# Turning the quantised GELU rows by DMA on SyncE's queue, with the second product one step later

## The reference, cut to what matters

```python
def activation_quant(x):
    scale = 127.0 / jnp.clip(jnp.max(jnp.abs(x), axis=-1, keepdims=True), EPS_Q)
    return jnp.clip(jnp.round(x * scale), -128, 127) / scale
def bit_linear(x, w, b, dim_in):
    x_norm = simple_rms_norm(x, dim_in)
    x_q = activation_quant(x_norm)
    w_q = weight_quant(w)                       # sign(w) * mean(abs(w))
    return jnp.einsum('bsd,od->bso', x_q, w_q) + b
h = bit_linear(x, w1, b1, DIM)
h = jax.nn.gelu(h, approximate=False)
return bit_linear(h, w2, b2, INNER)
```

## Time and profile before

| | us |
|---|---|
| median of 3 runs | 2112.15 (2109.58 to 2112.73) |
| the profiled execution | 2108.11 |
| its span, first to last instruction | 2106.3 |
| PE busy in the span | 1942.6 (92%) |
| VectorE busy | 1350.0 (64%) |
| ScalarE busy | 1079.6 (51%) |
| GpSimd busy | 431.5 (20%) |

### The profile page before, as it was taken

One profiled execution on the slowest core, in us unless ns is written; L12 is line 12 of the kernel. 1 busy time (PEld: TensorE's weight loads), 2 busy tenths in 40 slices (PEclk: granted clock), 3 DMA queues, 4 the chain that ended last, 5 costly groups with the idle time before them and its releaser, 6 DMA issues. The chain is left out here.

```text
span 2106.3 us, 30642 instructions
## 1 busy us (share of the span) xinstructions
PE 1942.6 (92%) x10514; PEld 1486.9 (71%) x10514; DVE 1350.0 (64%) x2408; ACT 1079.6 (51%) x2590; POOL 431.5 (20%) x515
## 2 busy tenths in 40 slices
PE   6999789999999999969999999999979978886898
PEld 5888667777777777757887778778768855553444
DVE  6777577777777777744424655554745438885886
ACT  4333266666766666652314321121324329994998
POOL 1111144444444444410000000000000002222111
PEclk9999899999999999989999999999999989997999
DMA  6776853333332330146433221223287422331121
GB/s 251 262 261 218 297 155 110 82 91 91 101 89 83 100 80 23 31 137 228 145 100 130 60 60 40 61 61 107 94 294 247 149 82 96 116 101 51 33 59 45
DMA packets 209028, 253.76 MB, mean 120 GB/s; under 512 B 12246, under 2 KB 158822, under 8 KB 202476
## 3 DMA queue, kind: packets, MB, share of 16 engines
q1 hardware_dynamic: 208876, 251.82, 37.2%
HBM read 151.10 MB, written 100.68 MB: 120 GB/s over the span
## 5 line engine op out<-in xcount | busy, mean ns | idle before, releaser
L971 ACT ACTIVATE at_prob<-at_S,at_bias,at_rq 128x384 f32<-128x384 f32 (+1 forms) x256 | 185.2, 733 | 131.5 <-DVE at_bias L1058 124.3
L1069 DVE TENSOR_TENSOR at_pt_lo<-at_PT,at_pt_hi 128x512 fp32r<-128x512 f32 x224 | 154.8, 692 | 84.6 <-ACT at_pt_hi L978 84.6
L835 POOL TENSOR_SCALAR at_prob<-at_prob,at_rsum 128x384 f32<-128x384 f32 (+1 forms) x256 | 161.4, 643 | 148.9 <-DVE at_rsum L1064 148.8
L1722 ACT ACTIVATE gu_silu<-gu_G 128x512 f32<-128x512 f32 x64 | 38.1, 597 | 242.7 <-PE gu_G L103 233.0
L1049 DVE TENSOR_REDUCE at_nmax<-at_S 128x1 f32<-128x384 f32 (+1 forms) x256 | 152.7, 619 | 6.6 <-PE at_S L885 2.3
L978 ACT ACTIVATE at_pt_hi<-at_PT 128x512 fp32r<-128x512 f32 x224 | 134.9, 603 | 42.3 <-PE at_PT L892 42.3
L1759 DVE TENSOR_TENSOR gu_h<-gu_silu,gu_U 128x512 f32<-128x512 f32 x64 | 43.9, 688 | 150.9 <-PE gu_U L103 104.0
L892 PE MATMUL at_PT<-c_ident,at_prob 128*128 128x128 f32 x896 | 126.0, 275 | 3.5 <-DVE at_pt_lo L1069 3.5
L824 POOL TENSOR_TENSOR at_q<-at_by_cos,at_by_sin 128x512 f32<-128x512 f32 x64 | 82.4, 1288 | 215.3 <-DVE at_qv L1044 183.3
L881 PE MATMUL at_S<-at_k_hi,at_q_hi 128*128 128x384 f32 (+1 forms) x256 | 109.7, 428 | 7.5 <-DVE at_q_lo L1074 7.5
L892 PEld LDWEIGHTS at_PT<-c_ident,at_prob 128*128 128x128 f32 x896 | 100.3, 140 | 22.4 <-DVE at_pt_lo L1069 14.2
(11 more groups left out here) (341 smaller groups left out, 5470.8 us busy)
## 6 DMA issues: line engine op xcount, KB each, us to landing
wide<-at_ot SPq DMA_DIRECT2D x64, 256.0 KB, 2.9
wide<-gu_h SPq DMA_DIRECT2D x64, 256.0 KB, 3.3
o_a<-wide SPq DMA_DIRECT2D x14, 1024.0 KB, 4.8
d_a<-wide SPq DMA_DIRECT2D x13, 1024.0 KB, 8.6
keys_hi<-kv_kt_hi SPq DMA_DIRECT2D x16, 512.0 KB, 3.2
keys_lo<-kv_kt_lo SPq DMA_DIRECT2D x16, 512.0 KB, 4.2
values_hi<-kv_v_hi SPq DMA_DIRECT2D x16, 512.0 KB, 4.8
values_lo<-kv_v_lo SPq DMA_DIRECT2D x16, 512.0 KB, 5.1
```

Source lines behind the costliest of these rows:

```text
L835: pool.tensor_scalar(prob[u % 2][:, h, 0:n], prob[u % 2][:, h, 0:n], rsum[:, s:s + 1], 1.0, ALU.mult, ALU.mult).then_inc(normed.sem, 1)
L971: act.activation(prob[u % 2][:, h, 0:n], S[h][:, 0:n], ACT.Exp, bias=bias[:, s:s + 1], scale=rq[u % 4][:, h:h + 1], accum_out=sums[:, s:s ...
L1069: dve.tensor_tensor(pt_lo[f % 4][:], bank_of("p", u, kb)[:], pt_hi[f % 4][:].bitcast(F32), ALU.subtract).then_inc(pt_done.sem, 1)
```

## The change

The rows of hq are no longer transposed on TensorE and copied out by ScalarE. SyncE issues a transposing DMA from hq to hqt (512 KB) for each tile, as the last item of its step, on tile s-2. `second_product` moves from tile s-2 to s-3, `finish` from s-3 to s-4, and `store_y` stays at s-4. xb gets eight rooms instead of four, used by the turn's parity, with a wait for the y that last read the room. The banks HT and their counters go.

```diff
-        xb = mem.sb("xb", [P, TT, D])
+        xb = mem.sb("xb", [P, 2 * TT, D])
-        HT = [mem.bank(f"HT{i}", (P, 1024), BF16) for i in range(2)]
-        HT_full = mem.counter("HT_full", 2 * TT)
-        ht_done = mem.counter("ht_done", 2 * TT)
+        hq_turned = [mem.counter(f"hq_turned{t}", 16) for t in range(TT)]
+        def xb_room(turn, t):
+            return xb[:, turn % 2 * TT + t, :]
 # SyncE
+            def turn_h(turn, t):
+                sp.wait_ge(*hq_done.at(turn, t + 1))
+                sp.wait_ge(*Y_full.at(turn, t + 1 - TT))
+                sp.dma_start_transpose(hqt[:, t, :, :], hq[:, t, :]).then_inc(hq_turned[t].sem, 16)
                 for a in back(4):
                     store_y(*a)
+                for a in back(2):
+                    turn_h(*a)
 # TensorE
-            def turn_h(turn, t):
-                pe.wait_ge(*hq_done.at(turn, t + 1))
-                for a in range(2):
-                    pe.wait_ge(*ht_done.at(turn, 2 * t + a - 1))
-                    for i in range(8):
-                        j = 8 * a + i
-                        last = pe.transpose(HT[a][:, i * P:(i + 1) * P], hq[:, t, j * P:(j + 1) * P], c.ident_bf[:])
-                    last.then_inc(HT_full.sem, 1)
             def second_product(turn, t):
                 pe.wait_ge(*y_done.at(turn, t))
+                pe.wait_ge(*hq_turned[t].at(turn, 16))
                 for k in range(IC):
-                    if k % 8 == 0:
-                        pe.wait_ge(*ht_done.at(turn, 2 * t + k // 8 + 1))
-                for a in back(2):
-                    turn_h(*a)
-                for a in back(2):
+                for a in back(3):
                     second_product(*a)
 # ScalarE
-            def keep_h(turn, t):
-                for a in range(2):
-                    act.wait_ge(*HT_full.at(turn, 2 * t + a + 1))
-                    if a == 0:
-                        act.wait_ge(*Y_full.at(turn, t + 1 - TT))
-                    act.activation(hqt[:, t, 8 * a:8 * a + 8, :].rearrange("p k q -> p (k q)"), HT[a][:],
-                                   ACT.Copy).then_inc(ht_done.sem, 1)
-                for a in back(2):
-                    keep_h(*a)
 # VectorE
-                dve.tensor_tensor(xb[:, t, :], x[:, t, :], b2g[:], ALU.add).then_inc(xb_done.sem, 1)
+                if turn > 0:
+                    dve.wait_ge(*y_done.at(turn - 1, t + 1 - TT))
+                dve.tensor_tensor(xb_room(turn, t), x[:, t, :], b2g[:], ALU.add).then_inc(xb_done.sem, 1)
-                dve.wait_ge(*HT_full.at(turn, 2 * (t + 1 - TT)))
+                dve.wait_ge(*hq_turned[t].at(turn, 0))
-                for a in back(3):
+                for a in back(4):
                     finish(*a)
```

More of the change, by code:

```diff
@@ L2323, in quantised_ffn @@
         ROWS = (0, 1, 2, 0, 1, 0)
+        def xb_room(turn, t):
+            return xb[:, turn % 2 * TT + t, :]
         @block.sync
         def _(sp):
-            for s in (*x_arrived, *y_stored):
+            for s in (*x_arrived, *hq_turned, *y_stored):
                 s.start(sp)
+            def turn_h(turn, t):
+                sp.wait_ge(*hq_done.at(turn, t + 1))
+                sp.wait_ge(*Y_full.at(turn, t + 1 - TT))
+                sp.dma_start_transpose(hqt[:, t, :, :], hq[:, t, :]).then_inc(hq_turned[t].sem, 16)
             def load_x(turn, t):
@@ L2380, in _ @@
         def _(pe):
-            for s in (XT_full, H_full, HT_full, Y_full):
+            for s in (XT_full, H_full, Y_full):
                 s.start(pe)
@@ L2433, in _ @@
         def _(act):
-            for s in (x_sq, xt_done, gelu_done, h_sq, h_scaled, ht_done):
+            for s in (x_sq, xt_done, gelu_done, h_sq, h_scaled):
                 s.start(act)
@@ L2586, in finish @@
                 dve.wait_ge(*y_stored[t].at(turn, 0))
-                dve.scalar_tensor_tensor(out=y[:, t, :], in0=Y[:], scalar=from_q[1][:, t:t + 1], in1=xb[:, t, :],
+                dve.scalar_tensor_tensor(out=y[:, t, :], in0=Y[:], scalar=from_q[1][:, t:t + 1], in1=xb_room(turn, t),
                                          op0=ALU.mult, op1=ALU.add).then_inc(y_done.sem, 1)
```

## The result

| | before | after |
|---|---|---|
| median, us | 2111.39 (4 runs, 2109.58 to 2112.73) | 2185.74 (4 runs, 2184.12 to 2189.7) |
| profiled execution / its span | 2108.11 / 2106.3 | 2184.55 / 2182.7 |

The ratio is 1.0355, with a 95% interval of 1.0338 to 1.0373: the change costs 74 us. Forecast were 2211 us within 2158 to 2305; direction and mechanism hold, the size was 25 us too high.

A forecast was written before the change was run, and what follows sets the result against it. ScalarE was taken as the bound, with TensorE and VectorE close under it. The SyncE loop adds 34.6 + 14 T, 99 us at T = 4.6, to 2112: 2211 us, range 2158 to 2305.

The forecast's parts named there:

- The bound and what little there was to gain: Steady last stage: ScalarE bounds, TensorE and VectorE close under it; gain at most 0.28 us a step, 4.5 us in all.
- Part 2, the loop: SyncE's load of x waits behind store_y for the same step's finish: step 12.55 + T us against 9.44.
- Part 3, T: What the transposing DMA on SyncE adds before the load can run as if alone: 4.6 us, up to 11.5.
- The plain bound: Lower end of T, by bytes: a plain 512 KB DMA costs the one behind it 1.4 us.
- the piece price: Upper end of T: 2048 pieces of 256 bytes at 0.06 us each over 16 engines, 7.7 us.
- Neither is nearer: Bytes like the cheap row, pieces smaller than any in the trace, so the middle was taken for T: 4.6 us.
- Part 4, place by place: Last stage's lateness at x(3), x(4), x(5) to x(15) and the drain: 34.6 + 14 T, 99 us.
- Cover: Hidden costs: turned tile's landing has 12 us of cover; TensorE's lower clock hidden by 3.8 us at T = 4.6.
- The profile after: x_statistics waits some 3 to 8 us for x; SyncE goes store, transposing DMA, load; ScalarE busy 31 us less; 17 us steps.
- (a): Rival: the transposing DMA's 16 blocks turned one after another, T = 22.4, 348 us more, 2460 us; chance 0.12.
- (b): Rival: load of x not late, VectorE bounds at 9.07 us a step, 4.5 us less, 2107.6 us; chance 0.03.
- (c): Rival: load of x is held, but early work by the freed ScalarE makes up for it, 2112 us; chance 0.02.

The follow-up runs named there:

- pe_order: Changed kernel with x loaded one SyncE step earlier, transposing DMA before the store, second Y bank, second product before first product: 2109.4 us.
- load_ahead: Changed kernel with each load of x issued one SyncE step earlier, ahead of the store and the transposing DMA: 2109.7 us.
- shift_only: Kernel before with only the later second product and finish and eight rooms for xb, no transposing DMA: 2150.1 us.
- plain_dma: Changed kernel with a plain DMA of the same 512 KB in place of the transposing one, rows left unturned: 2164.1 us.
- store_late: Changed kernel with the transposing DMA ahead of the store and the store one SyncE step later: 2157.5 us.
- turned_twice: Changed kernel with a second transposing DMA of the same hq into a spare tile ahead of each: 2225.3 us.
- no_shift: Changed kernel with x loaded one SyncE step earlier, transposing DMA before the store, second product at s-2, finish at s-3: 2108.4 us.

## Why the prediction was right, and where its size was off

- **The bound and what little there was to gain**: right. I gave at most 0.28 us a step. From x(5) on, the step fell from 9.36 to 9.02 with the loop open, by 0.34. VectorE's own pace, seen in pe_order, is 8.97, a little under my 9.07, with a wait of 0.44 us for GpSimd's power still in it. The 9.46 of the table is higher than 9.36 because it has the one step of 10.53 in it.
- **Part 2, the loop**: right in each link. load_ahead removes all of the loss; shift_only has the loop without any new DMA. Worked out 12.55 us at T = 0, measured 12.71.
- **Part 3, T**: this is the term that was mis-sized. I took 4.6, the middle of 1.4 and 7.7; the steps give 2.61, and 2.54 for a second one. The plain bound was itself too high (0.94, not 1.4). In the piece price the count was right (2080 packets for 2048 pieces), but a piece cost 0.024 us by the estimate above and not the kernel's mean packet of 0.06. By that price the pieces come to 3.1 us instead of 7.7. "Neither is nearer" was the wrong step: there were no grounds for the middle. Nor do the pieces stand apart from all before, as I wrote: the page of before counts 12246 packets under 512 B, without saying how small.
- **Part 4, place by place**: by the sum with T = 2.6, 34.6 + 14 x 2.6 = 71 us, where the stage in the trace grew by 73 and the medians by 74. x(3) to x(4) 9.2 + 2.6 = 11.8, measured 11.6. The eleven steps 34.2 + 11 x 2.6 = 63 more, measured 64. The drain 0.6 + 2.6 = 3.2 more, measured 4.5, and mostly for another reason: shift_only's drain is 3.3 longer without the DMA, which leaves 1.2 for it. My own items for the drain also add up to 20.6 and 22.3 us where I wrote 21.0 and 22.5. x(3) was late by 1.2 us against x(0) instead of 2.6: the step from x(1) to x(2) took 8.15 us instead of 9.59. plain_dma and store_late, which do the same work up to there, took 9.74 and 9.81 for it, so this isn't the change's doing. That x(3) and the drain err in opposite ways and nearly cancel is luck.
- **Cover**: TensorE's lower clock (0.84 on average) stayed hidden, as worked out. The tile's landing (4.6 us) did in the steady state; in the drain TensorE waits 2.5 us for it.
- **The profile after**: the order of SyncE's issues and the waits for x are as told, the latter 6.1 us a step. ScalarE's busy time fell by 28.5 us, where I had 31.
- **Rivals**: (a) blocks one after another, T = 22.4, is out; the Trainium skill's 1309 ns a block in "VectorE: DVE Perf Modes", section "The three transpose paths", taken 16 times, is an estimate of 20.9 us, where the whole DMA of 16 blocks landed in 4.6. The Trainium skill's other rule ("Advanced Engine Details and Errata", section "X-Bar Transpose (TRN2)"), that a transposing DMA is as fast as a regular one, does not hold for what it cost here: 2.61 us against 0.94. (b), the faster side, is what load_ahead shows to have been on offer: -1.6 us by the medians, within its uncertainty. (c), no change, is out by 74 us.

## What to carry to other kernels

When an instruction is moved by a step, look at who waits for it on an in-order DMA queue and what is queued behind that wait: here a load that lost its lead cost 36 us, with nothing slow in it. Put what is ready early before the wait, and loads ahead of both. The same transposing DMA cost 2.6 us a step behind the wait and nothing before it, as long as the wait that followed was there to cover it (store_late, without that wait, gained only 0.1 us a step). Taking 1.8 us off a bound engine is worth only the distance to the next engine, and here TensorE and VectorE both stood 0.3 to 0.4 us below it.

## What the runs showed of the hardware that I had not expected

A DMA_TRANSPOSE of a 128x2048 bf16 tile from SBUF to SBUF held SyncE's queue for 1.5 to 3.7 us (up to 3.9 in turned_twice), where a plain DMA of the same 512 KB held it for 0.47. It landed after 4.3 to 4.7 us against 3.5 (medians). In the changed kernel short holds go with long landings of the load behind: of its 11 steps, issue to issue was 1.69 us with a landing of 4.31 in one, 3.54 with 3.30 in the next. What sets the length of the hold was not tried. When the issues stood close, plain ones took longer too: 1.0 us instead of 0.34 for the store right behind a transposing DMA in no_shift.
